# Two units centred in one set of tiles, another cut of the hand-over, and gate products that VectorE no longer makes

## The chip, the cores and the metric

The kernel runs on one core of a Trainium2 chip. The metric is the device time of one execution in microseconds (us). Before the change the median of three runs is 3228.43 us (3227.1 to 3233.3). The profiled execution took 3220.84 us, with a span of 3219.0 us from its first to its last instruction.

## What is computed

The input x is an image of 256 x 256 positions with 32 channels, float32. Three "triangle" layers are followed by a Mamba layer, all float32:

```python
# each of three layers, on x[i, k, c]
g  = (x - mean) / sqrt(var + 1e-5)            # one mean and variance over the whole image, per channel
xn = layernorm32(g) * scale + bias            # over the 32 channels
L  = (xn @ Wl + bl) * sigmoid(xn @ Wlg + blg) # 64 wide, needed in a band |i - k| <= 4 only
R  = (xn @ Wr + br) * sigmoid(xn @ Wrg + brg) # 64 wide, everywhere
V[i, k, h] = sum_{d=-4..4} L[i+d, i, h] * R[i+d, k, h]
x += (layernorm64(V) @ Wo + bo') * sigmoid(xn @ Wog + bog)
# Mamba layer: sequences along the first image axis (256 steps), one per column
h = exp(dt * A) * h + dt * B * x ; y = sum_s h * C + D * x ; out = x + (y * silu(z)) @ W_out
```

(The order of the output product and the gate is regrouped in the kernel; what matters here is which tensors are made from which.)

## The kernel before

**Triangle layers.** The image lies in SBUF as 128 partitions (four groups g of 32 channels) by 16384 columns. 32 units n of 512 columns are the grain of the work. `plan()` writes an order by hand: a list STEPS, in each step of which every engine walks the kinds of work in one fixed order. For a unit n, step n has the centring (`c1` on TensorE, one 128x128 matrix `norm_w` against 512 columns into bank 0; `a1` on ScalarE, which copies bank 0 to `xn` with a bias and frees the bank; a square on GpSimd for the variance). Four units' variances are summed in step n//4*4+4 (`v1`), ScalarE forms rstd of eight units at once (`root1`), TensorE spreads it over the partitions (`bc1`) and VectorE multiplies `xn` with it, at the head of step n//2*2+10. In step n+11 comes the gate projection (`gate1`, banks 4 and 5, then a sigmoid on ScalarE), in step n+12 the value projection (`val1`, banks 2 and 3, then VectorE makes R). `project` uses tiles of 32 rows by 64 columns of the TensorE array: for gate n and value n-1, of opposite parity, the eight tiles are all different. SP's queue stores R to DRAM. GpSimd's queue loads windows of R back once units 0 to 15 are stored; from step 29 on the band products (`band`, 68 tiles) are made and stored. From step 44 on the outputs are formed (`a3`, `y1`, `y2`, `v3`, `root3`, `bc3`), GpSimd adds the result to x, and the next layer's statistics are gathered. The left factor (`left`, `lt`, steps 1, 2, 10 to 12, 14 to 16) is a small side chain of all engines, whose transposes use bank 1.

**Hand-over.** In the third layer SP stores each finished unit of x to DRAM (`store_x`), and `hand_over` reads x back as rows by columns for the Mamba layer, into the memory of `xn`: rows 0 to 127 by GpSimd's queue beside units 18 to 25; the rest when the stores of units 0 to 27, and then of 28 to 31, have landed, on ScalarE's, GpSimd's and SP's queues.

**Mamba layer.** 32 chunks of 8 columns (2 in each of 4 groups), 16 steps s each (8 groups of channels dg in two halves q). In a step TensorE spreads dt*x (`pb`, double buffered), VectorE multiplies it with B in PSUM and scans (`tensor_tensor_scan`), ScalarE makes the decay exp(dt*A) from rows that SP's queue loads, GpSimd multiplies the states with C, and TensorE adds them up in `py[q]`, LAG = 3 steps later, in program order between the spreads. `SHARES` says which other work stands after which step of an engine: PRE prepares the next chunk, OWN belongs to this chunk, POST finishes the one before. VectorE makes the gate product y*silu(z) of half 0 after step 11 and of half 1 after step 4 of the next chunk; TensorE's output product stands in step 7, VectorE's addition of x (`fin`) in step 8. GpSimd makes dt and dt*x of the next chunk after steps 7 to 11, ScalarE's queue stores the dt rows in step 14. Names used below: `sum_states` and `steps` (TensorE), `decay` (ScalarE), `gate` and `post` (VectorE).

## Time and profile before

| what | value |
|---|---|
| median of 3 runs | 3228.43 us |
| profiled execution / its span | 3220.84 / 3219.0 us |
| layers begin (statistics ready) at | 29, 440 and 844 us |
| end of the last hand-over load, about | 1322 us |
| 32 chunks of the scan | about 1360 to 3210 us |
| busy over the span: TensorE, VectorE, ScalarE, GpSimd | 82, 78, 59, 62 % |

A row of the view of groups gives a line, an engine, the tensors, the count, busy us, mean ns of one, and idle time in front with what ended it. A row of the timeline gives start and length in us; several like instructions are merged into one row with their count. A float32 matmul is recorded as two passes, so one matmul of a program line counts as two.

### The profile page before, as it was taken

Reading aid. Unit: us, or ns where it says so; the run is one execution under the profiler, and the core shown is the slowest. Engines: PE = TensorE matmul, PEld = TensorE weight load, DVE = VectorE, ACT = ScalarE, POOL = GpSimd, SP = SyncE. Lnnn points to the kernel's source line nnn. Section 1 sums busy time; section 2 is a strip of 40 time slices with the busy share of each in tenths; the row PEclk is TensorE's granted clock in tenths of the full one; section 3 lists DMA queues with packets and bytes.
Section 4 is the critical chain, followed back from the end, with each engine's and each line's share of the span. In section 5 each row is a group of like instructions: output and inputs, shape, how many; then the busy total and the mean of one; then the engine's idle time right before and its main releaser. Section 6 shows DMA issues by size and latency. Waiting matters only on the chain.

```text
span 3219.0 us, 39492 instructions
## 1 busy us (share of the span) xinstructions
PE 2640.8 (82%) x12378; PEld 791.6 (25%) x12378; DVE 2522.4 (78%) x2238; ACT 1897.1 (59%) x2340; POOL 1990.3 (62%) x1220
## 2 busy tenths in 40 slices
PE   5888888888888877388888888888888888888886
PEld 1233122331223311122222222222222222222221
DVE  4555555555555544399999999999999999999998
ACT  3524545335553344476776777767777677776772
POOL 2444234442344422178888788887888878878786
PEclk9989989999998999699999999999999999999998
DMA  3688315883159846575766767667676675766765
GB/s 144 206 286 247 104 39 188 311 248 107 40 169 311 256 135 157 113 170 142 179 154 154 168 143 177 155 153 170 141 175 159 149 173 139 175 158 151 173 142 118
DMA packets 257633, 537.45 MB, mean 167 GB/s; under 512 B 39544, under 2 KB 150592, under 8 KB 256624
## 3 DMA queue, kind: packets, MB, share of 16 engines
q1 hardware_dynamic: 211168, 442.96, 51.9%
q0 software_dynamic: 19040, 64.24, 7.4%
q10 hardware_dynamic: 27312, 28.79, 3.8%
q8 instruction: 66, 1.08, 0.1%
q14 instruction: 47, 0.39, 0.0%
HBM read 396.55 MB, written 139.33 MB: 166 GB/s over the span
## 4 chain that ended last, share of the span: by engine, by line
issue 19%; PE 18%; DVE 17%; ACT 2%; DMA 1%; POOL 1%; DVEq 1%; ACTq 0%; POOLq 0%
DVE m_pb L461 11%; PE m_pb L279 6%; PE m_py L262 5%; DVE m_hs L466 4%; PE m_misc L227 3%; PE m_misc L246 2%; PE m_py L258 1%; DVE m_gated L418 1%; PE m_misc L233 1%; ACT m_da L388 1%; DMA m_dtb<-dt_rows 1%; ACT m_xg L310 1%; POOL m_hs L492 1%; DMA dt_rows<-m_dt 0%; DVE m_fin L476 0%
## 5 line engine op out<-in xcount | busy, mean ns | idle before, releaser
L492 POOL TENSOR_TENSOR m_hs<-m_hs,m_cs 128x1024 f32<-128x1024 f32 x512 | 1205.3, 2359 | 383.9 <-DVE m_hs L466 383.9
L466 DVE TENSOR_TENSOR_SCAN m_hs<-m_da,m_pb 128x1024 f32<-128x1024 f32 x512 | 1170.9, 2287 | 29.2 <-ACT m_da L388 4.2
L279 PE MATMUL m_pb<-m_dtx,late 64*128 64x512 f32 x2048 | 597.3, 649 | 217.8 <-DVE m_hs L466 217.6
L388 ACT ACTIVATE m_da<-m_dtb,m_a_neg 128x1020 f32<-128x1020 f32 x512 | 579.5, 1143 | 284.2 <-DMA m_dtb<-dt_rows 206.4
L461 DVE TENSOR_TENSOR m_pb<-m_pb,m_bs 128x1024 f32<-128x1024 f32 x512 | 620.4, 1212 | 10.9 <-PE m_pb L279 10.5
L262 PE MATMUL m_py<-m_hs,late 128*64 128x512 f32 x2048 | 566.9, 632 | 62.4 <-POOL m_hs L492 62.2
L1442 POOL TENSOR_TENSOR t_xc<-t_xc,big 128x512 f32<-128x512 f32 x96 | 120.1, 1271 | 336.9 <-DVE big L1348 336.9
L279 PEld LDWEIGHTS m_pb<-m_dtx,late 64*128 64x128 f32 x2048 | 168.3, 188 | 617.6 <-DVE m_hs L466 547.3
L999 PE MATMUL t_bank<-late,t_lwin 128*128 128x256 f32 x816 | 224.9, 413 | 51.4 <-ACT big L1225 33.3
L1322 DVE SCALAR_TENSOR_TENSOR t_xc<-t_bank,t_vec,t_xc 128x512 f32<-128x512 f32 x96 | 72.0, 750 | 243.8 <-PE t_bank L1018 243.8
L1439 POOL TENSOR_TENSOR t_sq<-big 128x512 f32<-128x512 f32 x96 | 102.7, 1070 | 239.7 <-ACT big L1195 171.2
L1213 ACT ACTIVATE t_sq<-t_bank 128x512 f32<-128x512 f32 x192 | 105.5, 598 | 244.0 <-PE t_bank L1065 243.9
L1222 ACT ACTIVATE t_gate<-t_bank,t_small 128x512 f32<-128x512 f32 x192 | 121.5, 683 | 190.6 <-PE t_bank L1008 188.5
L1340 DVE SCALAR_TENSOR_TENSOR t_tile<-t_bank,t_small,t_gate 128x512 f32<-128x512 f32 x192 | 135.3, 746 | 107.7 <-issue 79.5
L262 PEld LDWEIGHTS m_py<-m_hs,late 128*64 128x64 f32 x2048 | 102.9, 137 | 473.7 <-issue 300.3
L1305 DVE TENSOR_TENSOR t_vwin<-t_bank,t_mask_k 128x512 f32<-128x512 f32 x204 | 139.5, 689 | 94.4 <-PE t_bank L999 75.7
L1374 POOL DMA_DIRECT2D late<-right_factor x96 | 56.9, 592 | 228.5 <-PE t_bank L999 157.9
L999 PEld LDWEIGHTS t_bank<-late,t_lwin 128*128 128x128 f32 x816 | 150.2, 198 | 174.4 <-issue 105.5
L380 ACT COPY m_cs<-m_misc 128x512 f32<-128x512 f32 x128 | 68.7, 589 | 193.6 <-PE m_misc L246 193.6
L1065 PE MATMUL t_bank<-t_tile,t_center 64*64 64x512 f32 x768 | 126.6, 669 | 63.9 <-DMA t_tile<-band_out 49.7
L310 ACT ACTIVATE m_xg<-big,m_gn_bias,m_gn_scale 64x512 f32 (+1 forms) x128 | 163.6, 1278 | 1.7
L246 PE MATMUL m_misc<-m_act,late 64*128 64x512 f32 x512 | 146.6, 649 | 13.0 <-ACT m_act L332 10.6
(164 smaller groups left out, 3629.2 us busy)
## 6 DMA issues: line engine op xcount, KB each, us to landing
m_dtb<-dt_rows SPq DMA_DIRECT2D x512, 512.0 KB, 6.1
late<-right_factor POOLq DMA_DIRECT2D x102, 512.0 KB, 5.7
right_factor<-t_tile SPq DMA_DIRECT2D x192, 256.0 KB, 2.9
t_tile<-band_out SPq DMA_DIRECT2D x183, 256.0 KB, 4.1
band_out<-t_vwin SPq DMA_DIRECT2D x48, 512.0 KB
band_out<-t_vwin SPq DMA_DIRECT2D x48, 480.0 KB
dt_rows<-m_dt ACTq DMA_DIRECT2D x64, 256.0 KB, 3.3
t_xc<-in_x_cm SPq DMA_DIRECT2D x4, 2048.0 KB, 14.6
```

What stands on the lines that cost most here:

```text
L246: nc.tensor.matmul(misc[n][:, :], w_bc[rows, b, :], act[par][rows, half(q)], start=True, stop=True).then_inc(misc_ready[n], 1)
L262: m = nc.tensor.matmul(py[q][D * n:D * n + D, :], gather[:, dg, :], hs[:, s % H_RING, half(n)], start=False, stop=(dg == DG - 1), skip_gro ...
L279: m = nc.tensor.matmul(pb[s % 2][:, half(n)], spread[rows, dg, :], dtx[par][rows, half(q)], start=True, stop=True)
L310: m = nc.scalar.activation(xg[par][P // 4 * shift:P // 4 * shift + P // 2, q, :, first:first + T], xm[rows, :, bass.ds(SUB * k, SUB)].rear ...
L388: nc.scalar.activation(da[:, s % DA_RING, :, 1:T], dtb[s % DTB_RING][:, :].rearrange("p (r t) -> p r t", t=T)[:, :, 1:T], ACT.Exp, scale=a ...
L461: nc.vector.tensor_tensor(pb[s % 2][:, :], pb[s % 2][:, :], bs[q][:, :], ALU.mult).then_inc(u_done, 1)
L466: nc.vector.tensor_tensor_scan(hs[:, s % H_RING, :], da[:, s % DA_RING, :, :].rearrange("p r t -> p (r t)"), pb[s % 2][:, :], 0.0, ALU.mul ...
L492: nc.gpsimd.tensor_tensor(hs[:, s % H_RING, :], hs[:, s % H_RING, :], cs[q][:, :], ALU.mult).then_inc(hc_ready, 1)
L999: m = nc.tensor.matmul(bank[b][:, e * COLS:(e + 1) * COLS], lwin[:, slot, LROW * h + BAND:LROW * h + BAND + P], rwin[:, slot, h * COLS:(h ...
L1065: m = nc.tensor.matmul(bank[p][o:o + HID, :], center64[HID * hs:HID * hs + HID, HID * hs:HID * hs + HID], tile[HID * hs:HID * hs + HID, sl ...
L1305: nc.vector.tensor_tensor(vwin[:, slot, UNIT * j:UNIT * j + UNIT].rearrange("p (h k) -> p h k", k=COLS), bank[b][:, :].rearrange("p (h k) ...
L1340: nc.vector.scalar_tensor_tensor(tile[:, at[key], :], bank[2 + p][:, :], bias[:, 1:2], gate[:, at[l, "sig", n, p], :], ALU.add, ALU.mult). ...
```

## The change

Four edits. (1) `center` replaces the 128x128 centring matmul of a unit by four 32x32 tiles; the tiles of an even unit lie on the diagonal of the array, those of the odd unit beside it are shifted by two column groups, so its groups land swapped in `xn`, and `project` follows that. Two units are centred at the end of one odd step into banks 0 and 1. (2) `bc1` and its product move from the head to the end of a step (for steps below 31) with banks 7 and 0; gate, value, band and output steps all move one step later; the left factor's transposes use bank 7. (3) The hand-over is cut in other pieces. (4) In the Mamba layer ScalarE copies `py` to `gated` (`take`) and GpSimd multiplies it with silu(z) there; `out` moves from step 7 to 8 on TensorE and from 8 to 9 on VectorE; for the first chunk VectorE makes half of the shifted copies of x.

```diff
-            "tensor": {... 5: [(PRE, "dt")], 8: [(PRE, "z")], 7: [(POST, "out")], ...
+            "tensor": {... 5: [(PRE, "dt")], 8: [(PRE, "z"), (POST, "out")], ...
-            "scalar": {1: [(PRE, "silu_x")], 3: [(OWN, "bq1")], 5: [(OWN, "cq1")],
+            "scalar": {1: [(PRE, "silu_x")], 3: [(OWN, "bq1")], 4: [(POST, "take1")], 5: [(OWN, "cq1")],
-                       ... 12: [(PRE, "cq0")],
+                       ... 12: [(PRE, "cq0"), (OWN, "take0")],
-            "vector": {4: [(POST, "gate1")], 8: [(POST, "out")], 11: [(OWN, "gate0")]},
-            "gpsimd": {7: [(PRE, "loss0"), (PRE, "log0")], ...
+            "vector": {9: [(POST, "out")]},
+            "gpsimd": {5: [(POST, "gate1")], 13: [(OWN, "gate0")], 7: [(PRE, "loss0"), (PRE, "log0")], ...
...
+                def take(k, par, q):                       # ScalarE
+                    a.wait_ge(hc_used, S * k + DG * (q + 1))
+                    if q == 0 and not early(k, 1):
+                        a.wait_ge(o_ready, k)
+                    nc.scalar.copy(gated[:, half(q)], py[q][:, :]).then_inc(y_taken, 1)
...
-                        for shift in (0, 2):
+                        for shift in (0,) if early(k, 1) else (0, 2):
...
+                def first_xg(q):                           # VectorE, chunk 0
+                    ...
+                    nc.vector.tensor_scalar(xg[0][P // 2:P, q, :, 1:1 + T], xm[rows, :, 0:SUB].rearrange("p t n -> p n t"),
+                                            gn_scale[rows, 0:1], gn_bias[rows, 0:1], ALU.mult, ALU.add).then_inc(xg_first, 1)
...
-                            if q == 0:
-                                pe.wait_ge(y_gated, 2 * k - 1)
+                            if q == 0:
+                                pe.wait_ge(y_taken, 2 * k - 1)
...
+                def gate(k, par, q):                       # GpSimd
+                    g_.wait_ge(y_taken, 2 * k + q + 1)
+                    g_.wait_ge(misc_used[q], use(k, "z") + 1)
+                    nc.gpsimd.tensor_tensor(gated[:, half(q)], gated[:, half(q)], act[par][:, W + q * HALF:W + (q + 1) * HALF],
+                                            ALU.mult).then_inc(y_gated, 1)
...
-        A3_STEP = [44 + n if n < 14 else 46 + n for n in A3]
+        A3_STEP = [45 + n if n < 14 else 47 + n for n in A3]
...
-                for kind, lag in (("a1", 0), ("gate1", 11), ("val1", 12)):
+                for kind, lag in (("a1", 0), ("gate1", 12), ("val1", 13)):
                     steps[n + lag][kind].append(n)
+                steps[max(n // 2 * 2 - 1, 0)]["c1"].append(n)
...
-            where = [s for k, s in zip(per_step, range(29, 41)) for _ in range(k)]
-            where += [45 + t // 3 for t in range(32)] + [56, 56, 57, 57]
+            where = [s for k, s in zip(per_step, range(30, 42)) for _ in range(k)]
+            where += [46 + t // 3 for t in range(32)] + [57, 57, 58, 58]
...
         def band_bank(t):
...
-            return (1, 7, 0)[j] if tile_step[t] < A3_STEP[0] else (7, 2, 3)[j]
+            return ((1, 7, 0) if tile_step[t] >= LAST_C1 else (0, 7))[j] if tile_step[t] < A3_STEP[0] else (7, 2, 3)[j]
 
         def bc1_bank(n):
-            return (7, 1 if n < 22 else 0)[n % 2]
+            return (7, 0)[n % 2]
+
+        LAST_C1 = 31
...
-        X_GROUP = lambda n: 0 if n < 16 else 1 if n < 28 else 2
+        X_GROUP = lambda n: 0 if n < 16 else 1 if n < 24 else 2 if n < 28 else 3
...
-                sp.wait_ge(x_stored[2], 16 * 4 * 4)
+                hand_over(sp, first_row(16, 1), 8 * 28)
+                sp.wait_ge(x_stored[3], 16 * 4 * 4)
                 hand_over(sp, first_row(28, 0), first_row(16, 1))
...
+                def center(l, n):
+                    wait_bank(n % 2, (l, "c1", n))
+                    for g in range(4):
+                        o = C * (g ^ 2 * (n % 2))
+                        m = nc.tensor.matmul(bank[n % 2][o:o + C, :], norm_w[C * g:C * g + C, C * g:C * g + C], x_unit(n)[C * g:C * g + C, :],
+                                             start=True, stop=True, skip_group_check=True)
+                    m.then_inc(full[n % 2], 1)
...
-                        for n in st["a1"]:
-                            wait_bank(0, (l, "c1", n))
-                            nc.tensor.matmul(bank[0][:, :], norm_w[:, :], x_unit(n), start=True, stop=True).then_inc(full[0], 1)
...
                             project(l, "val", n, w_r, 2)
+                        for n in st["bc1"] if s < LAST_C1 else ():
+                            spread_rstd(l, n)
+                        for n in st["c1"]:
+                            center(l, n)
...
-                a.wait_ge(x_stored[1], 16 * 4 * 12)
-                hand_over(a, P, first_row(28, 0))
-                hand_over(a, first_row(16, 1), 8 * 28, (2, 3))
                 a.wait_ge(x_stored[2], 16 * 4 * 4)
-                hand_over(a, 8 * 28, ROWS, (2, 3))
+                hand_over(a, first_row(24, 0), first_row(28, 0))
+                a.wait_ge(x_stored[3], 16 * 4 * 4)
+                hand_over(a, 8 * 28, ROWS)
...
+                            if l == LAYERS - 1 and n in (26, 27):   # GpSimd
+                                g_.wait_ge(x_stored[1], 16 * 4 * 8)
+                                hand_over(g_, P, first_row(24, 0), (2 * n - 52, 2 * n - 51), shared.x_in_pool)
...
-                g_.wait_ge(x_stored[1], 16 * 4 * 12)
-                hand_over(g_, first_row(16, 1), 8 * 28, (0, 1), shared.x_in_pool)
-                g_.wait_ge(x_stored[2], 16 * 4 * 4)
-                hand_over(g_, 8 * 28, ROWS, (0, 1), shared.x_in_pool)
```

## Rows read from the trace of the kernel before

**Rows 1.** Busy time by stretch: stretch, length, PE, PEld, DVE, ACT, POOL, clock, DMA share, GB/s.
```profile
436.00:843.00 407.00, 342.36 (x2332) 117.78 (x2332) 227.94 (x359) 190.78 (x310) 159.27 (x150) 0.95 0.55 178
1996.10:2053.71 57.61, 49.43 (x169) 13.58 (x169) 56.80 (x36) 41.50 (x46) 47.37 (x25) 0.97 0.68 160
1310.00:1320.00 10.00, 0.00 (x0) 0.00 (x0) 0.00 (x0) 0.00 (x0) 1.56 (x2) 0.50 1.18 215
```

**Rows 2.** Groups of instructions in two chunks of the scan, 1996.10 to 2111.33.
```profile
L492 POOL TENSOR_TENSOR m_hs<-m_hs,m_cs 128x1024 f32<-128x1024 f32 x33 | 77.8, 2362 | 20.2 <-DVE m_hs L466 20.2
L511 POOL TENSOR_TENSOR m_dtx<-m_dt,m_act 128x512 f32<-128x512 f32 x4 | 5.1, 1272 | 0.0
L380 ACT COPY m_cs<-m_misc 128x512 f32<-128x512 f32 x8 | 4.3, 589 | 13.7 <-PE m_misc L246 13.7
L418 DVE TENSOR_TENSOR m_gated<-m_py,m_act 128x512 f32<-128x512 f32 x4 | 2.7, 666 | 0.0
```

**Rows 3.** Timeline of one chunk: start, length, engine, line, [idle before].
```profile
2025.92 2.35 POOL L492 TENSOR_TENSOR m_hs<-m_hs,m_cs 128x1024 f32<-128x1024 f32 x1 [1.08 <-DVE m_hs L466]
2040.50 0.67 DVE L418 TENSOR_TENSOR m_gated<-m_py,m_act 128x512 f32<-128x512 f32 x1
2041.08 1.22 DVE L461 TENSOR_TENSOR m_pb<-m_pb,m_bs 128x1024 f32<-128x1024 f32 x1
2047.57 6.97 POOL L492 TENSOR_TENSOR m_hs<-m_hs,m_cs 128x1024 f32<-128x1024 f32 x3
2052.26 2.58 ACT L310 ACTIVATE m_xg<-big,m_gn_bias,m_gn_scale 64x512 f32 x2
```

**Rows 4.** The same timeline, over the border to the next chunk.
```profile
2052.63 1.08 PE L262 MATMUL m_py<-m_hs,late 128*64 128x512 f32 x4
2053.64 3.70 PE L227 MATMUL m_misc<-m_xg,m_w_conv 128*128 128x512 f32 x8
2057.27 1.13 PE L279 MATMUL m_pb<-m_dtx,late 64*128 64x512 f32 x4
2058.45 1.23 DVE L461 TENSOR_TENSOR m_pb<-m_pb,m_bs 128x1024 f32<-128x1024 f32 x1
```

**Rows 5.** Timeline of TensorE in layer two, from its start to the first band product.
```profile
443.67 2.06 PE L1039 MATMUL t_bank<-t_xc,t_norm_w 128*128 128x512 f32 x2
448.55 1.78 PE L954 MATMUL t_bank<-t_xc,t_norm_w 32*32 32x144 f32 x32
458.57 1.12 PE L1039 MATMUL t_bank<-t_xc,t_norm_w 128*128 128x512 f32 x2 [0.78 <-ACT big L1195]
474.09 1.98 PE L1008 MATMUL t_bank<-big,t_w_rg 32*64 32x512 f32 x8 [0.68 <-ACT late L1161]
...
545.63 2.07 PE L999 MATMUL t_bank<-late,t_lwin 128*128 128x256 f32 x4 [4.09 <-DMA late<-right_factor]
```

**Rows 6.** Timeline of TensorE in layer two, two steps with gate and value projections.
```profile
518.08 0.66 PE L1008 MATMUL t_bank<-big,t_w_r 32*64 32x512 f32 x4
...
520.58 0.66 PE L1008 MATMUL t_bank<-big,t_w_rg 32*64 32x512 f32 x4 [0.36 <-ACT t_gate L1222]
520.90 0.66 PE L1008 MATMUL t_bank<-big,t_w_r 32*64 32x512 f32 x4
521.92 1.13 PE L1035 MATMUL t_bank<-t_rstd,t_sel 32*128 32x512 f32 x4
524.03 0.66 PE L1008 MATMUL t_bank<-big,t_w_rg 32*64 32x512 f32 x4
```

**Rows 7.** Groups of instructions in 443 to 535 us, layer two.
```profile
L1439 POOL TENSOR_TENSOR t_sq<-big 128x512 f32<-128x512 f32 x27 | 28.3, 1049 | 62.6 <-ACT big L1195 37.4 <-PE t_bank L1093 25.2
...
L1294 DVE TENSOR_TENSOR late<-late,t_lwin 128x1152 f32<-128x1152 f32 x2 | 2.7, 1355 | 0.0
```

**Rows 8.** Timeline: the first copies of x in the Mamba layer, the last gate product.
```profile
1329.31 5.04 ACT L310 ACTIVATE m_xg<-big,m_gn_bias,m_gn_scale 64x512 f32<-64x512 f32 x4
3211.74 0.69 DVE L418 TENSOR_TENSOR m_gated<-m_py,m_act 128x512 f32<-128x512 f32 x1 [4.49 <-PE m_py L262]
```

More of the change, by code:

```diff
@@ L181, in share @@
             def share(k, par, kinds, s):
-                table = FIRST if kinds == (PRE,) and k == -1 and name in FIRST else SHARES
+                table = FIRST if kinds == (PRE,) and k == -1 and name in FIRST else FIRST_X if isinstance(k, int) and k == -2 and name in FIRST_X else SHARES
                 for kind, op in table[name].get(s, []):
@@ L1011, in project, with spread_rstd @@
                         if g % 2 == 1:
-                            m.then_inc(full[first + g // 2], 1)
+                            m.then_inc(full[first + p], 1)
+                def center(l, n):
[5 more added lines that the diff above has]
+                    m.then_inc(full[n % 2], 1)
+                def spread_rstd(l, n):
+                    rows, i = rstd_rows(l, "root1", n)
+                    cg = 32 * (i % 4)
+                    b = bc1_bank(n)
+                    wait_bank(b, (l, "bc1", n))
+                    nc.tensor.matmul(bank[b][:, :], sel1[cg:cg + 32, i // 4, :], rows[cg:cg + 32, :],
+                                     start=True, stop=True).then_inc(full[b], 1)
                 def output(b, n, mat, halves):
@@ L1311, in _ @@
                     for s, st in enumerate(STEPS):
-                        for n in st["bc1"]:
-                            b = bc1_bank(n)
-                            v.wait_ge(full[b], use[l, "bc1", n])
-                            nc.vector.tensor_tensor(xn_unit(n), xn_unit(n), bank[b][:, :], ALU.mult).then_inc(free[b], 1)
+                        for n in st["bc1"] if s >= LAST_C1 else ():
+                            normalize(l, n)
                         for _ in st["weights"]:
```

131 lines of the change are left out of this document (68 added, 63 removed).

## The prediction

> **What bounds the kernel now.** I read the busy time by stretch first. A reader sees two different kernels in it [rows 1]. In layer two, 407 us long, no engine is full: TensorE is busy for 342 us, VectorE for 228, ScalarE for 191, GpSimd for 159, DMA for 55% of the time. In a chunk of the scan, 57.61 us long, VectorE is busy for 56.80 us, so there VectorE is the bound, and what leaves it counts, until something else is late. After 1300 us comes a stretch in which the engines stand and the DMA rings are full (share 1.18), the end of the hand-over [rows 1]. Then I took the groups of the scan for the price of each instruction [rows 2], one chunk of the timeline for the second bound behind VectorE [rows 3, 4], and TensorE's timeline of a layer [rows 5, 6] for its three phases: a fill from the first centring at 443.67 to the first gate projection at 474.09 (30.4 us), 16 steps and a DMA round trip up to the first band product at 545.63 (71.5 us), then bands and outputs.
>
> The sum is made against the profiled execution (3220.84 us, span 3219.0). It lies 7.6 us under the median of 3228.43; I take the gain off the median unchanged.
>
> **Scan: what leaves VectorE.** Two gate products per chunk go. Their rows are 0.67 us long, but what counts is from start to start: the product at 2040.50 is followed by the next spread product at 2041.08, so one costs 0.58 us [rows 3], two 1.16 us per chunk. They come back as a copy of 0.59 us on ScalarE each and a product of 1.27 us on GpSimd each (the price of the same shape there) [rows 2]. Busy time per chunk becomes 41.5 + 1.2 = 42.7 us on ScalarE and 47.4 + 2.5 = 49.9 us on GpSimd, of about 56.7 [rows 1]. Both have room on average; the question is where the products stand.
>
> Half 1 (the old place is after step 4, the new one on GpSimd after step 5). GpSimd waits more than 1 us before every state product in that part (1.08 us before the one at 2025.92) [rows 3], and is 1.27 us longer there once: the next product is about 0.2 us late, the one after it not at all. TensorE reads a state product one step after that, so nothing is late. ScalarE's copy after step 4 stands ahead of a decay that is needed two steps later. This gate is worth its full 0.58 us.
>
> Half 0 (old: after step 11). From step 7 on GpSimd has eight more products (dt and dt*x of the next chunk) and runs without a gap: from 2025.92 through the three state products that start at 2047.57. The second of these (step 13) ends at 2047.57 + 2 x 2.32 = 2052.2 [rows 3]. TensorE's sum of that product was at 2052.63, behind it the next chunk's x (3.63 us), then the spread at 2057.27, and VectorE took that one at 2058.45 [rows 4]. Without the gate VectorE would be there 0.58 us sooner, but the state product of step 13 is made at the same time after step 7 as before, so the sum can start at 2052.25 at best: 0.38 us sooner. That is what is late next, and I take 0.38 for this gate. The gate itself stands behind that product on GpSimd, after step 13; behind it are the state products of steps 14 and 15, which it makes 1.27 us later. Their sums stand in TensorE's queue behind the spread that starts at about 2057, when both but the last are ready, so this costs nothing; by the second step of the next chunk GpSimd has caught up (it needs 2.36 us [rows 2] of each step of 56.7/16 = 3.5 us). A third chain has to be watched: dt rows to DRAM and back, the decay of the next step 0, then the copies of x from 2052.26 to 2054.84 [rows 3]. TensorE needs the second of them 1.8 us after the start of its x work, at 2055.1 in the new order: 0.2 us of room. `out` one step later puts about 1 us of matmul behind z instead of a step ahead of it; the spread for step 9 stands behind it, but VectorE takes a spread only about two steps after the scan that frees its bank, and TensorE is busy for 49.4 of 57.6 us [rows 1], so I cost it at nothing; `fin` one step later changes nothing on VectorE's sum.
>
> Gain per chunk 0.58 + 0.38 = 0.96 us, for 30 chunks 28.8; the first and last chunk, without that second bound, 1.7: 30.5 us. The drain pays: the last gate product, 0.69 us at 3211.74 [rows 8], becomes 0.59 + 1.27 with a hand-over, 1.3 us more. The first chunk: ScalarE makes two copies of x ahead of TensorE's first work instead of four for both halves (5.04 us for four) [rows 8]; TensorE starts one copy, 1.25 us, sooner. Scan in all: 30.4 us. Bounds: 0.58 us per chunk only (18 us) if GpSimd's chain is stiffer than I read it, 1.16 us (37 us) if it has slack that I don't see.
>
> **Layers, the fill.** Now a centring takes 1.12 us and then waits 0.78 us for ScalarE to empty the only bank [rows 5]: 1.9 us for a unit. In the new order two units stand in two banks. If their eight tiles run side by side, 16 passes take what 2 rounds take. The projections show that they can: the gate's eight passes start at 520.58, the value's eight at 520.90, and the next matmul comes at 521.92 [rows 6], so 16 passes of 32x64 tiles take about 1.1 us, no more than 2 passes of the full array. For a pair: 1.1 us TensorE, two copies on ScalarE, and next two squares of 1.05 us on GpSimd [rows 7], which are late next. About 2.5 us for two units instead of 3.8, for some 8 units: 5.2 us. I take 5; bounds 0 (the left factor's chain through ScalarE and VectorE sets the fill) and 9 (all 11 units at GpSimd's 1.05 us).
>
> **Layers, the steps with projections.** A pair of steps now costs TensorE four full passes (1.06 for the spread of rstd, 2 x 1.06 for the centring), 2 x 1.05 for the projections, and half of a variance sum, 0.5: 5.8 us, against a spacing of 5.95 us (518.08 to 524.03) [rows 6]. The change takes 1.06 of it. But a second bound is near: value projections of successive steps are at 518.08 and 520.90 [rows 6], and nothing but the loop value projection, VectorE's product, freed bank lies between them: 2.82 us a step. So a pair costs 5.64 us at least and gains 0.3 to 0.5, not 1.06. ScalarE's rstd work with its two table loads holds the sigmoids back twice in these 16 steps, before as after. More comes at the start: the left factor's masks on VectorE (three of 1.36 us [rows 7]) now stand in a step that has a gate projection but no value product behind them, worth about 2 us. Over the 16 steps: 2 + 7 x 0.4 = 4.8, from which I take off 0.8 for the new wait that the centring's bank 0 has to be freed by VectorE's product with rstd, which stands behind the value product: 4 us. Bounds: -3 (that wait in each pair) and 16 (1.06 for each pair of units). The step that is added everywhere costs nothing by itself: the first gate projection moves by one step, the last by one, the work is the same. The first band product follows the value of unit 15 by a DMA round trip (TensorE waited 4.09 us for it [rows 5]), and this stays. Bands and outputs keep their order.
>
> 5 + 4 = 9 us per layer, 27 us for three.
>
> *A rule against this.* The row first: 32 passes of 32x32 tiles with 144 columns, four row groups into one bank, started at 448.55 and took 1.78 us [rows 5]; one after the other, at the pace of the rows with 512 columns (0.53 us a pass, so 0.15 for 144), they would take 4.8 us. So they do overlap in one bank. The Trainium skill, "TensorEngine Tiling (Array Packing)", section "Gotcha 1: PSUM Pressure", says that different row tiles cannot access the same bank at the same time. By that rule a pair would take longer than before; it is the third rival below. By this row the trace does not agree with it.
>
> **Hand-over.** In the stretch where the rings are full [rows 1] some 128 rows of x come back; the last loads land near 1322. The change puts 32 of these rows on GpSimd's queue some 6 us sooner, where the rings are half idle, and 32 behind SP's last store. At 32 KB a row and 215 GB/s [rows 1] 32 rows are 4.9 us. GpSimd pays for it: four issues of about 0.8 us each stand between its last additions to x, whose stores everything waits for. I take 3 us; bounds -3 and 6.
>
> **Sum.** 30.4 + 27 + 3 = 60.4 us: 3228.4 - 60.4 = 3168 us.
>
> **The rivals.**
> Only the scan gains. The layers stay at 407 us, since the loops through ScalarE and VectorE (2.82 us a step) and the DMA round trip set them, and the fill is set by the left factor. For it: no engine is full in a layer; against it: the 0.78 us behind each centring is plain waiting. 3228.4 - 31 = 3197 us.
> TensorE's work is the bound in full. 48 pairs of units x 1.06 = 51 us, and the scan gains 1.16 per chunk: 3228.4 - 51 - 37 - 4 = 3136 us. For it: TensorE's 8.4 us in 10 in a layer; against it: the 2.82 us loop and GpSimd's gapless run.
> Slower: the four row tiles of one unit go one after the other into their bank. A pair then takes 8 x 0.53 = 4.2 us instead of 2.1: +2.1 x 48 = 101 us; the 34 us of scan and hand-over remain: 3228 - 34 + 101 = 3295 us. It decides the sign once a pair takes more than 2.12 + 34/48 = 2.8 us. Against it: the row with 32 passes.
> The gates on GpSimd are no gain for half 0, and the dt chain loses its 0.2 us of room: scan 18 us less a little, layers as forecast, 3181 us.
>
> **How the numbers follow.** Forecast (3155 to 3182 by itself) 0.60; only the scan 0.12; TensorE in full 0.12; half 0 worth nothing 0.11; slower 0.03; no effect that can be measured 0.02. The range takes in all but the outer parts of the two wide rivals: 3143 to 3193 us. About 0.2%, 6.5 us, is what a measurement of this kernel can tell from no change. Faster 0.95, same 0.02, slower 0.03.
>
> **What would show it.** Chunk length 56.6 to 56.7 us (old 57.61), with no idle on VectorE but some 0.2 to 0.3 us before the second spread product of a chunk, released by TensorE. 16 passes of centring in 1.1 us for a pair. From a layer's first centring to its first gate projection 25 us instead of 30.4, from there to the first band product 67 to 68 instead of 71.5. The end of the hand-over about 3 us sooner relative to the last addition. Wrong would be: a chunk of 57 us or more, passes of centring that follow each other at 0.5 us, or TensorE waiting for VectorE's product with rstd in each pair.

## The result, and the profile after

The changed kernel takes 3129.66 us (median of 4 executions, 3125.4 to 3136.6) against 3228.56 us for the kernel before on the same chip: ratio 0.969, 95% interval 0.968 to 0.971, so 99 us less. The forecast was 3168 with a range of 3143 to 3193: the direction was right, the size too small by 38 us. On a second chip the same kernel gave 0.972 (0.970 to 0.975); this run stands below, among the scan's experiments.

Busy time by stretch in the kernel after; columns as in [rows 1]. The lines are layer two, one scan chunk, and layer two's stretch of bands (first band product to first output gate).

```profile
408.00:798.00 390.00, 325.64 (x2524) 111.08 (x2524) 226.77 (x357) 189.64 (x310) 159.74 (x150) 0.95 0.58 185
1995.00:2051.80 56.80, 49.96 (x170) 13.13 (x168) 55.69 (x34) 42.06 (x47) 49.76 (x27) 0.97 0.69 161
504.50:576.10 71.60, 60.59 (x388) 30.73 (x393) 47.37 (x72) 22.16 (x33) 37.56 (x39) 0.95 0.93 323
```

The same stretch of bands in the kernel before, which the prediction had not looked at:

```profile
545.60:623.80 78.20, 66.48 (x394) 32.61 (x398) 48.26 (x72) 22.96 (x34) 38.63 (x40) 0.91 0.85 296
```

It is 6.6 us shorter after. TensorE's clock and the DMA share are both higher, and neither row says which is the cause.

TensorE in layer two after (timeline, columns as in [rows 5]): the gate projection of unit 0, a value projection, two units' centring, the first band product.

```profile
439.93 1.09 PE L1031 MATMUL t_bank<-big,t_w_rg 32*64 32x512 f32 x8
...
472.99 1.09 PE L1041 MATMUL t_bank<-t_xc,t_norm_w 32*32 32x512 f32 x16
...
504.46 2.07 PE L1021 MATMUL t_bank<-late,t_lwin 128*128 128x256 f32 x4 [5.33 <-DMA late<-right_factor]
```

The first centring of the layer was at 415.51. So the fill, from the first centring to the first gate projection, takes 24.4 us (30.4 in [rows 5]), and it is 64.5 us from there to the first band product (71.5). The 16 passes of a pair take 1.09 us: the tiles run side by side, four row groups into one bank.

The scan at the border between two chunks, timelines of GpSimd, TensorE and VectorE:

```profile
2030.14 1.29 POOL L506 TENSOR_TENSOR m_gated<-m_gated,m_act 128x512 f32<-128x512 f32 x1
...
2030.25 1.08 PE L265 MATMUL m_py<-m_hs,late 128*64 128x512 f32 x4 [0.17 <-POOL m_hs L500]
2031.26 3.81 PE L230 MATMUL m_misc<-m_xg,m_w_conv 128*128 128x512 f32 x8
2035.00 1.13 PE L282 MATMUL m_pb<-m_dtx,late 64*128 64x512 f32 x4
...
2036.17 1.23 DVE L472 TENSOR_TENSOR m_pb<-m_pb,m_bs 128x1024 f32<-128x1024 f32 x1 [0.30 <-PE m_pb L282]
```

The sum waits 0.17 us for GpSimd's state product, x and the spread follow, and VectorE is idle for 0.30 us, in the place that the prediction named. In the view of one tile (`m_hs` on VectorE) the state scans, durations in ns and then first and last start, stand so; kernel before:

```profile
L466 DVE TENSOR_TENSOR_SCAN m_hs<-m_da,m_pb x512: 2286/2287/2289, 1366.0 to 3205.0; 128x1024 f32<-128x1024 f32 x171
```

Kernel after:

```profile
L477 DVE TENSOR_TENSOR_SCAN m_hs<-m_da,m_pb x512: 2285/2287/2290, 1295.6 to 3108.3; 128x1024 f32<-128x1024 f32 x171
```

That is 1839.0 against 1812.7 us, 0.85 us for each of 31 chunk lengths; below I call it the length of the scan. In the two traces layer one gives 28.2 us, layer two 16.0, layer three with the hand-over 24.8, the start of the Mamba layer 1.4, the scan 26.3, and the drain takes 1.3 back.

### The profile page after: what moved, and what is told of

Same layout as the page of the kernel before. It is cut to its first block, busy times and chain, and to the rows that moved or that the text cites. A ratio compares the mean times of both kernels' runs of the same rounds, so it can differ in the third digit from the quotient of the medians.

```text
span 3123.6 us, 40760 instructions
## 1 busy us (share of the span) xinstructions
PE 2573.1 (82%) x12954; PEld 756.1 (24%) x12954; DVE 2485.6 (80%) x2176; ACT 1914.4 (61%) x2402; POOL 2065.3 (66%) x1284
## 4 chain that ended last, share of the span: by engine, by line
POOL 29%; issue 27%; PE 5%; DVE 2%; DMA 2%; ACT 1%; SPq 1%; POOLq 0%; ACTq 0%; DVEq 0%
POOL m_hs L500 18%; POOL m_sp_v L517 2%; POOL m_dtx L527 2%; POOL m_gated L506 2%; DMA t_tile<-band_out 1%; POOL m_dt L524 1%; POOL m_dt L520 1%; SPq L913 1%; DVE m_pb L472 1%; PE t_bank L1096 1%; PE t_bank L1057 1%; PE t_bank L1021 1%; POOL t_xc L1481 1%; DVE m_hs L477 1%; PE m_misc L230 0%
## 5 line engine op out<-in xcount | busy, mean ns | idle before, releaser
L282 PE MATMUL m_pb<-m_dtx,late 64*128 64x512 f32 x2048 | 583.5, 646 | 150.2 <-DVE m_hs L477 146.9
L1021 PE MATMUL t_bank<-late,t_lwin 128*128 128x256 f32 x816 | 217.3, 404 | 63.3 <-ACT big L1260 34.0
L249 PE MATMUL m_misc<-m_act,late 64*128 64x512 f32 x512 | 147.1, 651 | 13.6 <-ACT m_act L343 11.1
```

The costliest lines, as they stand in the source:

```text
L249: nc.tensor.matmul(misc[n][:, :], w_bc[rows, b, :], act[par][rows, half(q)], start=True, stop=True).then_inc(misc_ready[n], 1)
L282: m = nc.tensor.matmul(pb[s % 2][:, half(n)], spread[rows, dg, :], dtx[par][rows, half(q)], start=True, stop=True)
L1021: m = nc.tensor.matmul(bank[b][:, e * COLS:(e + 1) * COLS], lwin[:, slot, LROW * h + BAND:LROW * h + BAND + P], rwin[:, slot, h * COLS:(h ...
```

## Experiments

### The three parts alone

*The scan's edits alone*, on the kernel before.
```diff
-            "vector": {4: [(POST, "gate1")], 8: [(POST, "out")], 11: [(OWN, "gate0")]},
+            "vector": {9: [(POST, "out")]},   # with take, gate on GpSimd, first_xg as in the change
```


> Kernel before with the scan's edits alone (gate products by ScalarE's copies and GpSimd, `out` one step later, two copies of x in the first chunk by VectorE). Own theory, from the two traces: the scan's gain is independent of the layers: 31 chunks by 0.85 us, 1.4 us at the start, 1.3 us lost at the end: 26 us less than before, between 24 and 29. Rival (part of the scan's gain in the changed kernel comes from elsewhere, for instance the chip's clock after the shorter layers): 20 us or less. By the prediction's rival with VectorE's full 1.16 us per chunk: 37 us.

0.9914 (0.988 to 0.995), 28 us less; length of the scan 1811.9 us.

*The layers' edits alone.*
```diff
+                steps[max(n // 2 * 2 - 1, 0)]["c1"].append(n)   # with center, banks, shifted steps
```


> Kernel before with the layers' edits alone (centring in pairs of units in two banks, rstd spread behind the value projection, first gate projection one step later), hand-over and scan as before. Own theory: the gain of the layers comes from these edits, the bands' part of it too: 28 us in layer one, 16 in two, about 20 in three: 60 to 67 us less than before. Rival (the bands' and outputs' gain, 23 us over the layers, is not from these edits but from the state of the rings or the clock): 40 us less. As predicted on record: 27 us less.

0.9814 (0.978 to 0.985), 60 us less (48 to 72).

*The hand-over alone.*
```diff
+                hand_over(sp, first_row(16, 1), 8 * 28)         # with X_GROUP in four groups
```


> Kernel before with the other pieces of the hand-over alone. Prediction on record: 3 us less (bounds 3 more, 6 less). From the traces the third layer with the hand-over gained 24.7 us where layer two gained 16.0 and layer one 28.2, so between 0 and 8 us less by what the layers gave without it; if the centring and scan parts measured beside it sum to the whole gain of 99 us, this one is within 2 us of nothing.

0.9972 (0.9955 to 0.9989), 9 us less (3.6 to 14.5). 28 + 60 + 9 = 97 us: the parts add up to the whole. The layers hold 33 of the 37 us that the sum missed, the hand-over 6; the scan gave 2 less than forecast.

### The layers: packing, order, or the shift

*Full centring matmul in the new order.* Only the packing is taken back (and `project` takes the groups of an odd unit as before).
```diff
-                    for g in range(4): ... norm_w[C * g:C * g + C, C * g:C * g + C] ...
+                    m = nc.tensor.matmul(bank[n % 2][:, :], norm_w[:, :], x_unit(n), start=True, stop=True)
```


> Changed kernel, but each centring is one product with the full 128x128 matrix again, still two units in a row in banks 0 and 1 and in the new order. Theory A (TensorE's time counts in full): a pair costs 1.06 us more, 16 pairs in each of three layers: 51 us more than the changed kernel. Theory B (the order and the second bank bring the gain, the loops through ScalarE and VectorE and the DMA set the pace): 5 to 15 us more than the changed kernel. Prediction on record: the packing's share is the 1.06 us in the fill (5 pairs, about half of it hidden) and 0.3 to 0.5 us in the steps: about 5 us a layer, 15 in all.

0.9774 (0.974 to 0.981). Without the scan's 28 and the hand-over's 9 its layers give some 36 us, so the packing's 1.06 us of a pair is worth about 24 of the 51 us that 48 pairs by 1.06 us would be. Against the changed kernel's own two ratios it is 16 to 26 us: far less than the 51 us of theory A, and rather more than the 5 to 15 of theory B. Stretches of layer two, from the first centring to the first band product, and the bands:

```profile
435.90:530.20 94.30, 81.65 (x576) 27.55 (x576) 48.01 (x78) 60.30 (x96) 38.91 (x42) 0.97 0.37 120
530.20:601.40 71.20, 59.41 (x390) 30.43 (x395) 47.62 (x72) 22.19 (x33) 38.41 (x39) 0.95 0.94 326
```

The first is 5.3 us longer than after (89.0), the bands are as short as after. So the bands' gain is not the packing's.

*Last centrings ahead of the bands*, on the kernel before.
```diff
+                    steps[min(n, 28) if kind == "a1" else n + lag][kind].append(n)
```


> Kernel before, but the centrings of units 29, 30 and 31 (with ScalarE's copy and GpSimd's square of each) stand in the loop's step 28 in place of steps 29 to 31, so ahead of the first band product. Own theory for the bands' gain: TensorE waited 4.1 us for the DMA ahead of the first band product, and the last centrings, which stood behind that wait, cost 1.1 us each there in full; ahead of it they are hidden. From the first band product to the first output gate some 5 us shorter than 80.5/78.1/78.6, the first band product 0 to 2 us later, in all 9 to 15 us less than the kernel before. Rival one (the bands' gain comes from the clock that TensorE is granted, 0.89 to 0.91 before and 0.93 to 0.97 after): no change in the bands and 0 to 5 us more in all. Rival two (the place of the rstd spread behind the value projection gives it): no change here, and a loss in the kernel measured beside it.

1.0030 (1.0016 to 1.0044): 10 us more, bands 80.9 to 82.1 us. My theory did not hold in this form. GpSimd's and TensorE's timelines show one reason. In GpSimd's queue the squares stand ahead of the loads of R's windows; here four squares in a row push the second load back, from 3.2 us behind the first (543.84 after 540.67 in the kernel before) to 9.6. TensorE's wait for a load, 4.09 us ahead of the first band product in the kernel before, is not gone: it now stands inside the bands.

```profile
540.89 0.61 POOL L1374 DMA_DIRECT2D late<-right_factor  x1 [4.17 <-DMA right_factor<-t_tile]
...
546.54 4.04 POOL L1439 TENSOR_TENSOR t_sq<-big 128x512 f32<-128x512 f32 x4 [3.40 <-PE t_bank L1093]
550.51 0.60 POOL L1374 DMA_DIRECT2D late<-right_factor  x1
...
556.32 2.08 PE L999 MATMUL t_bank<-late,t_lwin 128*128 128x256 f32 x4 [4.25 <-DMA late<-right_factor]
```

*Last centrings behind the wait for the DMA*, on the changed kernel.
```diff
+                late = n >= 29
-                for kind, lag in (("a1", 0), ...
-                steps[max(n // 2 * 2 - 1, 0)]["c1"].append(n)
+                for kind, lag in (("a1", int(late)), ...
+                steps[n if late else max(n // 2 * 2 - 1, 0)]["c1"].append(n)
```


> Changed kernel, but the centrings of units 29, 30 and 31 stand one to two steps later (at the ends of steps 29, 30 and 31), with ScalarE's copies and GpSimd's squares a step later too, so that two of them are behind the wait for the DMA ahead of the first band product. Theory A (part of the bands' gain is that the last centrings are ahead of that wait): first band product within 1 us of the same time, the bands 2 to 4 us a layer longer at the same clock, 6 to 12 us more in all. Theory B (the clock alone made the bands shorter): within 2 us of the changed kernel.

0.9755 (0.974 to 0.977) against 0.9723 (0.970 to 0.975) for the changed kernel on the same chip: 10 us more by the ratios, but the intervals overlap. Its bands are only 1.2 us a layer longer than those of the changed kernel at the same clock (the line of clock and length is below), less than the 2 to 4 us of theory A.

*Spread of rstd at the head of the step again.*
```diff
-                        for n in st["bc1"] if s < LAST_C1 else ():
+                        for n in st["bc1"] if s < 0 else ():      # and "if s >= 0" at the head
```


> Changed kernel, but the products that spread rstd, and VectorE's products with them, stand at the head of each step again, as in the kernel before. Theory A (their new place behind the value projection matters, since the odd unit's spread now shares bank 0 with the centring and waits there for ScalarE's copy): 5 to 20 us more than the changed kernel. Theory B (only the pairing of the centrings matters): within 3 us of it. Bands part: if rival two for the bands holds, it is 5 us a layer longer here.

0.9883 (0.985 to 0.991): 52 to 61 us more than the changed kernel (by its two ratios), far past both theories. Bands 69.2 to 70.0 us, even shorter, but 110.5 to 114.2 us from centring to band product instead of 88.7 to 90.8. In layer two TensorE is busy for 97.7 us of the 114.2, where the changed kernel has 72.9 of 88.9 for nearly the same instructions (771 and 768). The granted clock there is 0.79 against 0.96; 72.9 us scaled by it would be 88.6, so by this estimate some 16 of the 25 us are the clock (last section), and the rest stays open.

*Spread of rstd one step later.*
```diff
-                steps[n // 2 * 2 + 10]["bc1"].append(n)
+                steps[n // 2 * 2 + 11]["bc1"].append(n)
```


> Changed kernel with each pair's rstd spread one step later, so that they stand to the bands as in the kernel before; the centrings as changed. Theory A1 (of the 5 us a layer the spreads' place makes the greater part: in the trace of before the spread of the last pair waited 2.4 us for VectorE, which waited 3.2 us for a store of the bands): bands 2 to 4 us a layer longer, 6 to 12 us more in all than the changed kernel. Theory A2 (the centrings and the squares and window loads behind them make it): within 3 us of it.

0.9963 (0.995 to 0.998), some 78 us more than the changed kernel: more than the layers' whole gain. The bands are 2.1 us a layer longer at equal clock, but the loss stands before them: in 445 to 550 us TensorE waits so (waits: who, for whom, us in total, times, longest):

```profile
PE t_bank L1041 <- DVE big L1336: 16.1, 10, 1.7
```

The odd unit's spread and centring share bank 0; in one step the centring has to wait for VectorE's product with rstd. The prediction had bounded this wait (in each pair, -3 us a layer); it comes only with this order, and is more. In the changed kernel the same view of its 422 to 504 us has that wait once, for 1.7 us.

*Only the plan's shift*, on the kernel before: projections, bands and outputs stand one step later; centring, banks and places in the step are old.
```diff
-        A3_STEP = [44 + n if n < 14 else 46 + n for n in A3]
+        A3_STEP = [45 + n if n < 14 else 47 + n for n in A3]
...
-                for kind, lag in (("a1", 0), ("gate1", 11), ("val1", 12)):
+                for kind, lag in (("a1", 0), ("gate1", 12), ("val1", 13)):
...
-            where = [s for k, s in zip(per_step, range(29, 41)) for _ in range(k)]
+            where = [s for k, s in zip(per_step, range(30, 42)) for _ in range(k)]
...
```


> Kernel before, with only the layers' plan shifted: projections, bands and second half one step later, while centrings and rstd spreads stay in their steps (one unit at a time with the full matrix, old banks, old places in the step). Theory A (at the same clock the bands' 5 us a layer come from where the last centrings, squares and rstd spreads now stand relative to the bands): bands 4 to 6 us shorter than 80.5/78.1/78.6, 12 to 18 us less in all, or some us less than that if the first band comes later by the added step. Theory B (the gain needs the second bank or the spreads behind the value projection): bands as before, in all 0 to 9 us more than before by one more step of 2.8 us a layer.

0.9894 (0.988 to 0.991), 34 us less (29 to 40), twice what its own theory expected. Layer two, up to the first band product and the bands:

```profile
429.80:530.40 100.60, 84.95 (x578) 27.20 (x578) 49.32 (x80) 61.07 (x96) 41.52 (x42) 0.96 0.36 113
530.40:598.20 67.80, 59.49 (x388) 30.31 (x392) 46.31 (x70) 22.30 (x33) 37.49 (x39) 0.98 0.96 341
```

The bands take 67.8 us instead of 78.2. Of these 10.4 us, 7.0 are TensorE's busy time (66.48 to 59.49) and 3.4 its idle time. Six passes fewer stand there (388 instead of 394), some 3.2 us at 0.53 us each; the rest of the busy time goes with the granted clock, 0.98 instead of 0.91. Whether the shift brought that clock too is not shown. The rings are busy for 0.96 of the time instead of 0.85. What stood between the old bands is seen in their timelines, TensorE's first, then GpSimd's and VectorE's:

```profile
552.79 1.13 PE L1039 MATMUL t_bank<-t_xc,t_norm_w 128*128 128x512 f32 x2
...
557.21 1.02 PE L1039 MATMUL t_bank<-t_xc,t_norm_w 128*128 128x512 f32 x2
...
609.81 1.70 PE L1035 MATMUL t_bank<-t_rstd,t_sel 32*128 32x512 f32 x2 [2.44 <-DVE t_vwin L1305]
...
547.00 0.59 POOL L1374 DMA_DIRECT2D late<-right_factor  x1
...
554.72 1.04 POOL L1439 TENSOR_TENSOR t_sq<-big 128x512 f32<-128x512 f32 x1 [5.49 <-ACT big L1195]
555.70 0.59 POOL L1374 DMA_DIRECT2D late<-right_factor  x1
...
608.97 0.69 DVE L1305 TENSOR_TENSOR t_vwin<-t_bank,t_mask_k 128x512 f32<-128x512 f32 x1 [3.17 <-DMA band_out<-t_vwin]
```

Two centrings stand between the bands, and the square behind the first of them stands ahead of GpSimd's next window load (555.70, 8.7 us after the one before it). At 609.81 the last spread of rstd waits 2.4 us for a band's bank, which VectorE frees late because it waits 3.2 us for a store of the bands. Shifted by a step, one centring and the first of six pairs of spreads are done ahead of the first band product. The other spreads wait half as long. TensorE's waits in the bands of layer two, kernel before:

```profile
PE t_bank L1035 <- DVE t_vwin L1305: 7.5, 7, 2.4
PE t_bank L999 <- DMA late<-right_factor: 5.0, 3, 4.1
```

Only the shift:

```profile
PE t_bank L1035 <- DVE t_vwin L1305: 3.7, 4, 1.3
PE t_bank L999 <- DMA late<-right_factor: 5.8, 2, 4.1
```

So the idle time that went is that of the spreads. The waits for loads did not fall: behind the first one TensorE lost only 0.9 us to loads in the old bands, so the late load of 555.70 cost it little. How the 12 us a layer divide is only bounded by the kernels with a late centring (1.2 us a layer) and late spreads (2.1 us).

*One step more still*, on the best kernel below.
```diff
+        A3_STEP = [46 + n if n < 14 else 48 + n for n in A3]   # lags 13 and 14, bands from step 31
```


> As the kernel beside it, and the layers' projections, bands and second half one more step later against centrings and rstd spreads. Theory A (what makes the bands longer is every centring, square and spread that stands in them; one more step takes one odd step's worth out): bands 1 to 4 us a layer shorter, first band product 0 to 3 us later: 5 us less to 5 us more in all. Theory B (parity decides: the spreads in the even steps of the bands wait less; one more step brings the old parity back): bands 2 to 5 us a layer longer, 10 to 25 us more in all.

0.9706 (0.968 to 0.973) against 0.9669 (0.965 to 0.969) beside it: 12 us more. By its total this falls to theory B, but the traces say otherwise: at equal clock the bands are as long as in the kernels with the changed layers, and the first band product comes 3.4 us a layer later. Theory A does not hold either, since one pair of spreads fewer in the bands made them no shorter. The spreads wait 5.2 to 7.7 us there, nearly as long as in the kernel before (7.1 to 7.5) and in the one with late spreads (6.8 to 7.7), where they stand in the same steps counted from the first band; in the changed kernel it is 3.4 to 4.8, and with only the shift 3.5 to 3.9. So where the spreads stand sets how long they wait, but this alone does not set the length of the bands.

Means over the traced layers (27 for the changed layers, from nine traces):

| layers | first centring to first band | bands | clock in the bands | bands against the changed layers at equal clock |
|---|---|---|---|---|
| old (9) | 103.4 us | 79.8 us | 0.90 | +5.4 us |
| shift only (3) | 100.8 | 67.9 | 0.96 | -2.9 |
| changed, full matmul (3) | 96.1 | 72.4 | 0.92 | -0.8 |
| changed (27) | 90.1 | 73.1 | 0.92 | 0 |
| early last (3), old order | 102.8 | 81.5 | 0.88 | +6.0 |
| late last (3) | 89.8 | 74.5 | 0.92 | +1.2 |
| spread later (3) | 110.4 | 76.7 | 0.89 | +2.1 |
| spread first (3) | 111.9 | 69.7 | 0.95 | -1.5 |
| shift two (3) | 94.1 | 74.3 | 0.90 | 0.0 |

The last column takes the line through the 27 changed layers: 75.9 us at a clock of 0.87, 70.2 at 0.97, with a scatter of 0.7 us. By this line, of the 6.7 us that the old bands are longer, 5.4 are the order and about 1.3 the clock. The line shows that length and clock go together; that the clock sets the length was not tried by itself.

### The scan's second bound

*Half 0's gate on VectorE again.*
```diff
+            "vector": {9: [(POST, "out")], 11: [(OWN, "gate0")]},   # ScalarE's take0 and GpSimd's gate0 go
...
```


> Changed kernel with the gate product of half 0 on VectorE again after step 11, half 1 on ScalarE and GpSimd. By the prediction half 1 is worth 0.58 us per chunk and half 0 0.38 us; the changed kernel shows 0.85 in all, so half 0 should be worth 0.27: 8 us more than the changed kernel, chunks of 57.04 us. Rival (half 0's gate is worth its full 0.58 us and half 1 less): 18 us more.

0.9742 (0.972 to 0.977), length of the scan 1823.2 us: 10.5 more than the changed kernel's 1812.7, 0.34 us a chunk for half 0 (forecast 0.38), or 0.30 against the changed kernel's trace from the same chip (1813.8). Half 1 is then the rest of 0.85, 0.51 to 0.55 (forecast 0.58). The ratio by itself (6 us more than the changed kernel's 0.9723) is not clear of that kernel's interval.

*GpSimd's second dt*x after step 15, gate of half 0 after step 14.*
```diff
-            "gpsimd": {5: [(POST, "gate1")], 13: [(OWN, "gate0")], ... 11: [(PRE, "dtx1")]},
+            "gpsimd": {5: [(POST, "gate1")], 14: [(OWN, "gate0")], ... 15: [(PRE, "dtx1")]},
```


> Changed kernel, with GpSimd's second dt*x product of the next chunk after step 15 in place of step 11, and the gate product of half 0 after step 14 in place of 13. TensorE waits 0.17 us per chunk for GpSimd's state product of step 13 and VectorE then 0.30 us for the spread. Own theory (the limit of the scan's gain is GpSimd's gapless run up to step 13): VectorE's wait falls by 0.17 to 0.2 us per chunk, the last 0.1 us stays behind TensorE's own work; 5 to 6 us less than the changed kernel. If all of the 0.3 us goes: 9 us less. Rival (the moved products now delay the state products of steps 14, 15 and 0 past what TensorE hides): 0 to 10 us more.

No gain: 0.972 (0.9695 to 0.974), length of the scan 1814.1. In 1500 to 3000 us TensorE waits for GpSimd's state products 43 times instead of 92, but another wait, 0.5 us in the changed kernel, has come up:

```profile
PE m_misc L230 <- ACT m_xg L321: 4.5, 15, 0.5
```

ScalarE's copies of x, which stand behind the decay that waits for the dt rows, are now as late as GpSimd was. This is the third chain that the prediction said had 0.2 us of room.

*Both chains taken away*: as before it, and the copies of half 1 ahead of that decay.
```diff
-                       13: [(NEXT2, "xg0")], 14: [(POST, "store"), (PRE, "dt_rows")], 15: [(NEXT2, "xg1")]},
+                       13: [(NEXT2, "xg0")], 14: [(POST, "store"), (PRE, "dt_rows"), (NEXT2, "xg1")]},
```


> Changed kernel with the moved products of GpSimd of the kernel before (second dt*x after step 15, gate of half 0 after step 14), and ScalarE's copies of x for half 1 after step 14 in place of step 15, so ahead of the decay that waits for the dt rows. Own theory (two chains end together at TensorE's work on x: GpSimd's state product, and the dt rows with the copies of x behind them; taking one away leaves the other): both gone, VectorE's wait of 0.3 us a chunk goes too: 6 to 9 us less than the changed kernel, and the scan from first to last state scan takes 1804 to 1807 us. Rival (the rest is TensorE's own 6 us of work in that step): within 2 us of it.

0.9668 (0.965 to 0.969). The changed kernel was run beside it:

> The changed kernel as it is, on the same chip as the three beside it. If the second call's kernels were slower only by their edits: 0.969 of the kernel before. If the clock that TensorE gets differs from execution to execution, as the traces of kernels with the same layers suggest (0.87 to 0.97 in the bands, and 69.7 to 76.8 us for them): up to 0.973, with layers' bands longer where the clock is lower and nothing else changed.

It gave 0.9723 (0.970 to 0.975); by medians 3127 against 3137 us. The length of the scan is 1802.4 instead of 1813.8 us. In 1500 to 3000 us no wait of VectorE is listed any more; in the changed kernel (result section's trace) there was this one:

```profile
DVE m_pb L472 <- PE m_pb L282: 8.9, 26, 0.6
```

Two chains ended close to each other: taking GpSimd's away alone gave nothing, taking both away pays. ScalarE's chain alone was not taken away.

*The last sum of a chunk off VectorE too*, by a copy on ScalarE and an addition on GpSimd after step 14.
```diff
-            "vector": {9: [(POST, "out")]},
+            "vector": {},                     # ScalarE 9: take_out, 15: store; GpSimd 14: out
```


> As the kernel before, and the last product that is no part of the scan leaves VectorE too: ScalarE copies the output projection out of its bank after step 9, GpSimd adds x after step 14, the store goes after step 15. VectorE's 1.05 us row costs 0.97 us from start to start, 31 times: 30 us less than the kernel before if VectorE stays the bound (35 to 38 us less than the changed kernel), chunks of 55.5 us. Rival (with VectorE that short the dt rows through DRAM, or GpSimd at 51 us of 55.5, end last): 5 to 20 us less than the changed kernel.

0.9866 (0.985 to 0.988), 53 us more than the changed kernel instead of 35 less. TensorE waits, in 1500 to 3000 us:

```profile
PE m_misc L249 <- ACT m_act L334: 77.0, 25, 4.1
```

The store in ScalarE's queue waits for GpSimd's addition, and behind it stand the next chunk's activations.

*The same addition after step 13.*
```diff
-            "gpsimd": {... 14: [(OWN, "gate0"), (POST, "out")], ...
+            "gpsimd": {... 13: [(POST, "out")], 14: [(OWN, "gate0")], ...
```


> The kernel with the last sum of a chunk off VectorE, but that sum on GpSimd after step 13 in place of 14, so that ScalarE, which waits for it before the stores, is not held up ahead of the next chunk's first steps. There TensorE waited 77 us in 25 chunks for ScalarE's activations of x. Own theory (that wait in ScalarE's queue was the loss): 20 to 30 us less than the changed kernel. Rival (GpSimd has no room for 1.5 us more in a chunk ahead of its steps 14 and 15): no better than the changed kernel.

0.9665 (0.9646 to 0.9683), median 3123 us; the wait for `m_act` is gone. Run once more:

> The kernel with the last sum on GpSimd after step 13, once more as it is, beside a version with another plan of the layers. Earlier trace: scan 27 us shorter than in the changed kernel, but the medians of executions lay only some 15 us apart. If the scan's gain is real: 0.963 to 0.967 of the kernel before.

0.9669 (0.965 to 0.969), median 3123. The scan's length is 1786.7 and 1793.9 us in the two traces, 9 to 16 us less than with both chains taken away, but the times are not told apart from that kernel's. Its ratios, from two other chips, lie 8 to 19 us under the changed kernel's two (0.969 and 0.972); on one chip with the changed kernel only the version without both chains was run, 10 us less by the medians.

## Why the prediction was off, step by step

- *The step that failed: "The step that is added everywhere costs nothing by itself ... the work is the same", with "Bands and outputs keep their order".* The amount of work is the same, but its place is not: centring and spreads kept their steps while bands and projections moved. The shift alone is 34 us (29 to 40), against nothing in the sum. With it both centrings leave the bands in the changed kernel (one of two with the shift alone), and the spreads there wait 3.4 to 4.8 us instead of 7.1 to 7.5. I priced the shift by its own length and did not read the bands' stretch. Why the bands shorten by as much as they do is shown only in part, as the experiments above say.
- *Where the layers' missing 33 us lie.* By the traces' means the bands give 6.7 us a layer, 20 in all, where the sum had nothing, and the part ahead of them 13.4 us a layer, 40 in all, where it had 27.
- *Fill and steps, 9 us a layer, 27 in all.* Mis-sized. The traces of before and after show 13.2, 13.0 and 13.6 us a layer (in layer two the fill is 24.4 us where 25 were forecast, then 64.5 where 67 to 68 were). On average the fill gives 6.4 us for the forecast 5, the steps 7.0 for 4. In layer two the first value projection follows its gate by 3.1 us instead of 5.95 (forecast 2 us less), and from the first value projection to the last it is 54.0 us instead of 58.4, 4.4 less where 2.0 were forecast. The loop of 2.82 us a step, taken for a bound of 5.64 a pair, was not a firm one: value projections at 474.80 and 480.30 are a pair of steps apart, 5.50 us. The wait for the product with rstd, feared in each pair, comes once. With the shift alone the steps already give 4.5 of the 7.0 us, and the fill costs 1.9 more.
- *The rest of the layers' edits* is about 26 us beside the shift (60 - 34). This split assumes that the two add; the changed layers without the shift were not run, and each of these differences of ratios carries 10 us of uncertainty or more. By the traces the part up to the first band product gains 10.7 us a layer more (100.8 to 90.1), and the bands give about half of it back (67.9 to 73.1). The packing is 16 to 26 us of it.
- *Tiles of one unit side by side in one bank.* Right: 16 passes in 1.09 us. The Trainium skill, "TensorEngine Tiling (Array Packing)", section "Gotcha 1: PSUM Pressure", says that different row tiles cannot access the same PSUM bank at the same time. The row at 472.99 does not agree: four row groups write into one bank there, and 16 passes take 1.09 us.
- *TensorE's work in full (3136 us).* Near the result by its number, but not by its mechanism: the packing gave 16 to 26 of 51 us, the scan 28 and not 37. The recorded range, 3143 to 3193 us, leaves out this rival's own time and also that of "only the scan" (3197), 0.24 of the chances together, though the text says that it takes in all but their outer parts.
- *The scan, 30.4 us.* 28 us by the times (17 to 38), 26.3 by the traces. Mechanism, place and order of the waits were as forecast; half 0 0.30 to 0.34 for 0.38, half 1 0.51 to 0.55 for 0.58 us a chunk. The drain cost 1.3 us, as forecast.
- *Hand-over, 3 us (bounds -3 and 6).* Mis-sized: 9 us alone (3.6 to 14.5). From the first output gate of layer three to the Mamba layer's first matmul the 14 traces with the new pieces have 291.1 us on average, the 5 with the old 297.6: 6.5 us. Which of the moved pieces gives it was not tried apart.

## What to carry over

When a plan written by hand is shifted against a part that stays, go through the stretch at its far end too: list what stands between its first and last product in either version, and in which queue a load is issued behind it. A shift of "no work" was worth 34 us here, the saved matmuls 16 to 26. And where two chains end together, relieve both in one version before calling a resource the bound; if a wait moves to another engine, look at what stands behind the waiting instruction in its queue.

## What the runs showed of the hardware

The granted clock of TensorE can differ with the order of nearly the same instructions: from the first centring to the first band product the trace with the spreads at the head of the step has 0.88, 0.79 and 0.86 in its three layers, the changed kernel's 0.99, 0.96 and 0.93. With the spreads at the head of the step (and only that changed), in layer two, 8 us a line:

```profile
486.00:494.00 8.00, 5.82 (x36) 1.56 (x36) 2.68 (x4) 6.51 (x9) 5.16 (x7) 0.91 0.90 241
494.00:502.00 8.00, 6.58 (x49) 1.22 (x48) 3.51 (x5) 3.11 (x5) 3.34 (x5) 0.50 0.41 125
...
518.00:526.00 8.00, 8.00 (x44) 1.76 (x44) 2.79 (x4) 3.81 (x5) 1.04 (x1) 0.50 0.34 120
```

The changed kernel in about the same part of its layer two:

```profile
470.00:478.00 8.00, 7.42 (x76) 2.00 (x80) 5.99 (x10) 4.97 (x9) 4.65 (x6) 1.00 0.88 277
478.00:486.00 8.00, 7.90 (x84) 1.62 (x76) 5.96 (x10) 6.86 (x10) 2.05 (x3) 1.00 0.54 185
```

At 0.50, the lower level of 1.2 GHz, TensorE is busy for all of 518 to 526 us with 44 instructions. Before the clock fell to it TensorE was not busier than in the changed kernel: 7.25, 7.15 and 7.93 of 8 us in 462 to 486 (clock 1.00, 0.84 and 0.94) and 5.82 in the next 8 (0.91), against 7.42 and 7.90 at a clock of 1.00 in the two rows above. The stretch from centring to band product of that layer is 25 us longer. Why this order is granted less stays open. Kernels with the same layers differ too: the bands had clocks from 0.87 to 0.97 and took 69.7 to 76.8 us, so a difference of 6.6 us in the bands between one trace of each of two kernels does not by itself show what an edit did there.
